# Attention of layer 2: maxima turned in a score bank, away from their own scores; three operand buffers, filled in small parts between the blocks

## The reference

```python
q = q * cos + rot(q) * sin
k = k * cos + rot(k) * sin
g = H // KV
k = jnp.repeat(k, g, axis=1)
v = jnp.repeat(v, g, axis=1)
sc = jnp.einsum('bhqd,bhkd->bhqk', q, k) / jnp.sqrt(jnp.float32(dh))
mask = jnp.where(jnp.tril(jnp.ones((L, L), bool)), 0.0, -1000000000.0)
p = jax.nn.softmax((sc + mask).astype(jnp.float32), -1).astype(q.dtype)
o = jnp.einsum('bhqk,bhkd->bhqd', p, v).transpose(0, 2, 1, 3).reshape(Bsz, L, D)
return o @ o_w + res
```

## Time and profile before

| | |
|---|---|
| median of 3 runs | 6356.77 us |
| the profiled run's own time | 6361.04 us |
| its span | 6359.4 us, mean granted clock 0.826 |
| PE, DVE, ACT, POOL busy | 4190.6, 3786.9, 2670.5, 2605.6 us |
| input stage of attention | about 3564 to 3646 us of the span |
| attention | about 3646 to 4520 us |

### The profile page before, as it was taken

The page is one execution under the profiler, slowest core; times in us unless marked ns, Lnnn a source line. Parts: engine busy times, 40 slices in busy tenths (PEclk is TensorE's granted clock), DMA queues, the critical chain, the costliest instruction groups (busy, mean ns, idle before and its releaser), DMA issues. The chain is left out here.

```text
span 6359.4 us, 49945 instructions
## 1 busy us (share of the span) xinstructions
PE 4190.6 (66%) x13472; PEld 1927.0 (30%) x13472; DVE 3786.9 (60%) x5402; ACT 2670.5 (42%) x3917; POOL 2605.6 (41%) x1948
## 2 busy tenths in 40 slices
PE   4443686095236883788888657777877667777774
PEld 1111233074123551233333333333332222222221
DVE  6999642012322222699999633333436669999987
ACT  3442331031105771566665323333426545454443
POOL 2665001602521004599999200000000057878775
PEclk7776787597558996899999878887888889888897
DMA  1000002121121101344444122222020033333334
GB/s 39 9 9 7 8 0 87 51 68 45 61 102 44 38 31 55 107 154 150 153 153 143 65 30 32 32 31 30 1 71 12 28 106 115 116 118 115 116 114 139
DMA packets 153467, 442.82 MB, mean 70 GB/s; under 512 B 27558, under 2 KB 51048, under 8 KB 149408
## 3 DMA queue, kind: packets, MB, share of 16 engines
q1 hardware_dynamic: 135264, 395.43, 20.4%
q0 software_dynamic: 17984, 44.91, 2.0%
HBM read 363.65 MB, written 77.07 MB: 69 GB/s over the span
## 5 line engine op out<-in xcount | busy, mean ns | idle before, releaser
L1498 ACT ACTIVATE mb_h<-m_dt,m_a_neg 128x512 f32<-128x512 f32 x1024 | 660.7, 681 | 678.5 <-DVE m_hc L1615 578.9
L1376 PE MATMUL mb_y<-m_hc,m_diag_y 128*128 128x512 f32 x1024 | 574.8, 698 | 261.4 <-DVE m_hc L1615 149.5
L1606 DVE TENSOR_TENSOR_SCAN mb_h<-mb_h,m_u 128x1024 f32<-128x1024 f32 x320 | 733.8, 2293 | 8.9
L1568 POOL TENSOR_TENSOR m_u<-m_bsb,m_xs 128x1024 f32<-128x1024 f32 x256 | 598.0, 2357 | 30.7 <-DVE mb_h L1606 30.7
L1568 POOL TENSOR_TENSOR m_u<-m_bsb,m_dtx 128x1024 f32<-128x1024 f32 x256 | 596.1, 2361 | 27.8 <-DVE mb_h L1606 26.6
L1376 PE MATMUL mb_y<-m_hc,w_common 128*128 128x512 f32 x1024 | 513.2, 641 | 136.9 <-DVE m_hc L1615 77.7
L2067 DVE TENSOR_REDUCE at_mx<-at_ps_s 128x4 f32<-128x512 f32 (+1 forms) x256 | 245.1, 957 | 523.7 <-PE at_ps_s L1866 523.6
L1555 POOL TENSOR_TENSOR m_hc<-m_hs,m_csb 128x1024 f32<-128x1024 f32 x192 | 452.2, 2355 | 244.0 <-DVE m_hs L1606 244.0
L1606 DVE TENSOR_TENSOR_SCAN m_hs<-mb_h,m_u 128x1024 f32<-128x1024 f32 x192 | 437.6, 2279 | 1.8 <-POOL m_u L1568 1.8
L1615 DVE TENSOR_TENSOR m_hc<-mb_h,m_csb 128x1024 f32<-128x1024 f32 x320 | 391.8, 1224 | 4.7 <-issue 0.4
L1376 PEld LDWEIGHTS mb_y<-m_hc,m_diag_y 128*128 128x128 f32 x1024 | 202.4, 213 | 622.4 <-DVE m_hc L1615 251.5
(11 more groups left out here) (461 smaller groups left out, 8902.5 us busy)
## 6 DMA issues: line engine op xcount, KB each, us to landing
m_bsb<-bc_rows SPq DMA_DIRECT2D x256, 512.0 KB, 4.8
m_csb<-bc_rows SPq DMA_DIRECT2D x256, 512.0 KB, 4.0
at_q<-q_parts SPq DMA_DIRECT2D x144, 128.0 KB
x_slots<-r1zeros SPq DMA_DIRECT2D x8, 1024.0 KB, 10.0
xg_xg<-x_slots SPq DMA_DIRECT2D x32, 256.0 KB, 2.6
y_slots<-xg_yo POOLq DMA_DIRECT2D x32, 256.0 KB, 2.3
kept_x<-r SPq DMA_DIRECT2D x2, 4096.0 KB, 12.9
x_slots<-r2zeros SPq DMA_DIRECT2D x8, 1024.0 KB, 10.0
```

Source lines behind the costliest of these rows:

```text
L1376: mm = nc.tensor.matmul(ps_y[:, h], weight, hc[:, q % RING, s], start=False, stop=g == GROUPS - 1 and s == SG - 1)
L1498: ins = nc.scalar.activation(ps_h[:, q % 2, s], dt[:, i % 2, h], ACT.Exp, scale=a_neg[:, n:n + 1])
L1568: nc.gpsimd.tensor_tensor(u[:, q % RING], bsb[:, n % RING], dtx[:, i % 2, h].unsqueeze(1).broadcast_to([P, SG, TILE]), ALU.mult).then_inc( ...
L1606: V.tensor_tensor_scan(flat(to), flat(ps_h[:, q % 2]), flat(u[:, q % RING]), 0.0, ALU.mult, ALU.add).then_inc(h_ready, 1)
```

## The change

`q9` and `k9` are made outside both stages, with three buffers in place of two. The fill of `k9` and the first fetch go into `attention_inputs`: the fetch in three parts of six transfers, behind the stores of tiles 6, 7 and 8. In `attention` a fetch is always issued in such parts. The first part of fetch 1 comes before all, the other two after the row transfers of blocks 0 and 1. Fetch j follows in three parts after the rows of blocks 4j - 7, 4j - 6 and 4j - 5.

The maxima are turned into the first bank of `ps_s` instead of `misc`. Each block's are turned 6 units before its first unit. The scores of an odd block are made at units 0, 1, 3 and 4 of the block two before it (before: 1, 3, 5, 7). `turn` now waits, for an even block, until VectorE has read the scores of key head 0 of the next block, which lay in that bank; and the next scores to go into that bank (key head 2 of the next block after an even block's turn, key head 0 after an odd block's) wait for ScalarE's copy. The waits that `misc` had forced on `turn`, `to_tokens`, `to_heads` and `project` go.

```diff
+ATT_PARTS = 9 * DH
+ATT_BUFS = 3
+def fetch_parts(sp, q9, k9, q_d, k_d, j, loaded, parts):
+    s = j % ATT_BUFS
+    for a in parts:
+        at = slice(3 * a * DH, 3 * (a + 1) * DH)
+        q_src = q_d[j, :, a].rearrange("(h d) t -> d h t", d=DH)
+        for b in range(3):
+            sp.dma_start(q9[at.start + b * DH:at.start + (b + 1) * DH, s], q_src).then_inc(loaded, 16)
+        k_src = k_d[j // 4, j % 4 * 32:j % 4 * 32 + 32, a].rearrange("(g d) t -> d g t", d=DH)
+        for b in range(3):
+            sp.dma_start(k9[(3 * b + a) * DH:(3 * b + a + 1) * DH, s], k_src).then_inc(loaded, 16)
@@ attention_inputs: vector, first instruction
+            V.memset(k9[64:96].rearrange("p j g t -> p (j g t)"), 1.0).then_inc(filled, 1)
...
@@ attention_inputs: sync, inside the loop over i
+                if 6 <= i < 9:
+                    if i == 6:
+                        sp.wait_ge(filled, 1)
+                        sp.wait_ge(k_out0, 16)
+                        sp.wait_ge(q_out0, 16)
+                    fetch_parts(sp, q9, k9, q_d, k_d, 0, loaded, range(i - 6, i - 5))
+            sp.wait_ge(loaded, 16 * 18)
...
@@ attention
-    scores_at = {first[n] + (2 * g + 1 if n % 2 else g): (n + 2, g) for n in range(BLK - 2) for g in range(NKV)}
-    turn_at = {first[n - 1] if n % 2 else first[n - 2] + 4: n for n in range(2, BLK)}
-    turn_at[first[0]] = 1
+    scores_at = {first[n] + (g + g // 2 if n % 2 else g): (n + 2, g) for n in range(BLK - 2) for g in range(NKV)}
+    turn_at = {first[n - 2] + 6: n for n in range(2, BLK)}
...
-        ps_m = misc[:, 0:64].bitcast(BF16)
+        ps_m = ps_s[:, 0, 0, 0:64].bitcast(BF16)
-        q9 = sb("q9", [P, 2, NH, TILE], BF16)
-        k9 = sb("k9", [P, 2, NKV, TILE], BF16)
...
-            return n // 4 % 2, n % 4 * P, n % 4 // 2 * T
+            return n // 4 % ATT_BUFS, n % 4 * P, n % 4 // 2 * T
@@ scores
-                    pe.wait_ge(loaded[slot], (n // 8 + 1) * LOAD)
+                    if n:
+                        pe.wait_ge(loaded[slot], (n // 4 - 1) // ATT_BUFS * LOAD + LOAD)
+                if n >= 2 and g == (2 if n % 2 else 0):
+                    pe.wait_ge(nm_copied, n)
@@ turn
-                if n == 1:
+                if n == 0:
+                    pe.wait_ge(max_ready, 2 * NKV)
+                elif n == 1:
                     pe.wait_ge(nm_copied, 1)
-                if n % 2 and n >= 3:
-                    pe.wait_ge(x_done, n - 2)
-                if n % 2 == 0 and n >= 2:
-                    pe.wait_ge(on_ready, n - 2) if n >= 4 else pe.wait_ge(nm_copied, n)
+                elif n % 2 == 0 and n + 1 < BLK:
+                    pe.wait_ge(max_ready, (n + 1) * NKV + 1)
@@ to_tokens, to_heads, project
-                if n % 2 and n + 2 < BLK:
-                    pe.wait_ge(nm_copied, n + 3)
-                if n % 2 == 0:
-                    pe.wait_ge(oh_ready, n) if n else pe.wait_ge(nm_copied, 3)
-                if n == BLK - 1:
-                    pe.wait_ge(x_done, n)
+                if n:
+                    pe.wait_ge(x_done if n % 2 else oh_ready, n)
-                if n % 2 and n + 3 < BLK:
-                    pe.wait_ge(nm_copied, n + 4)
-                if n % 2 and n + 1 < BLK:
-                    pe.wait_ge(on_ready, n + 2)
...
@@ sync
-            fetch(0)
-            fetch(1)
+            fetch_parts(sp, q9, k9, q_d, k_d, 1, loaded[1], range(1))
             for n in range(BLK):
                 slot, col, _row = place(n)
                 sp.wait_ge(nm_copied, n + 1)
-                if n >= 8:
-                    sp.wait_ge(c_ready, last[n - 8] + 1)
+                if n >= 4 * ATT_BUFS:
+                    sp.wait_ge(c_ready, last[n - 4 * ATT_BUFS] + 1)
                 for a in range(3):
                     sp.dma_start(q9[PARTS + a:PARTS + a + 1, slot, :, col:col + P], nmt[a * NH:(a + 1) * NH, n % 2])\
                         .then_inc(less[n % 2], 16)
-                if n % 4 == 1 and 4 < n and n // 4 + 1 < NT:
-                    fetch(n // 4 + 1)
+                if n < 2:
+                    fetch_parts(sp, q9, k9, q_d, k_d, 1, loaded[1], range(n + 1, n + 2))
+                j = n // 4 + 2
+                if n % 4 and j < NT:
+                    if n % 4 == 1 and j >= ATT_BUFS:
+                        sp.wait_ge(c_ready, last[(j - ATT_BUFS) * 4 + 3] + 1)
+                    fetch_parts(sp, q9, k9, q_d, k_d, j, loaded[j % ATT_BUFS], range(n % 4 - 1, n % 4))
```

More of the change, by code:

```diff
@@ L1658, with attention_inputs @@
 QPK = NH // NKV
-def attention_inputs(nc, w, h, q_d, k_d, v_all):
+ATT_PARTS = 9 * DH
[10 more added lines that the diff above has]
+            sp.dma_start(k9[(3 * b + a) * DH:(3 * b + a + 1) * DH, s], k_src).then_inc(loaded, 16)
+def attention_inputs(nc, w, h, q_d, k_d, v_all, q9, k9):
     D = 4
@@ L1676, in attention_inputs @@
         (block, q_in, k_in, v_in, q_turned, k_turned, q_added, q_part, q_less, q_split, k_added, k_part, k_less, k_split,
-         v_done, q_out0, q_out1, q_out2, q_out3, k_out0, k_out1) = ctx.enter_context(phase(
+         v_done, filled, q_out0, q_out1, q_out2, q_out3, k_out0, k_out1, loaded) = ctx.enter_context(phase(
              nc, "q_in k_in v_in q_turned k_turned q_added q_part q_less q_split k_added k_part k_less k_split "
-             "v_done q_out0 q_out1 q_out2 q_out3 k_out0 k_out1"))
+             "v_done filled q_out0 q_out1 q_out2 q_out3 k_out0 k_out1 loaded"))
         q_out = (q_out0, q_out1, q_out2, q_out3)
@@ L1791, in _, with attention @@
                 sp.wait_ge(done, NT // 4 // 2 * 16)
-def attention(nc, w, q_d, k_d, v_all, x):
+def attention(nc, w, q_d, k_d, v_all, q9, k9, x):
     BLK = N // P
-    PARTS = 9 * DH
+    PARTS = ATT_PARTS
     RANK = PARTS + 3
@@ L1837, in attention @@
         eyeb = sb("eyeb", [P, QPK, P], BF16)
-        (block, consts, filled, loaded0, loaded1, less0, less1, v_filled, s_ready, max_ready, chain, split, turned, nm_copied,
+        (block, consts, filled, loaded0, loaded1, loaded2, less0, less1, v_filled, s_ready, max_ready, chain, split, turned, nm_copied,
          c_ready, exp_ready, v_ready, ov_ready, tok_ready, rc_ready, on_ready, heads_ready, oh_ready, out_ready,
          x_done) = ctx.enter_context(phase(
-             nc, "consts filled loaded0 loaded1 less0 less1 v_filled s_ready max_ready chain split turned nm_copied "
+             nc, "consts filled loaded0 loaded1 loaded2 less0 less1 v_filled s_ready max_ready chain split turned nm_copied "
              "c_ready exp_ready v_ready ov_ready tok_ready rc_ready on_ready heads_ready oh_ready out_ready x_done"))
-        loaded, less = (loaded0, loaded1), (less0, less1)
+        loaded, less = (loaded0, loaded1, loaded2), (less0, less1)
         LOAD = 16 * 18
         def place(n):
-            return n // 4 % 2, n % 4 * P, n % 4 // 2 * T
+            return n // 4 % ATT_BUFS, n % 4 * P, n % 4 // 2 * T
         @block.tensor
@@ L1905, in values @@
                 for g in range(NKV):
-                    mm = nc.tensor.matmul(ps_v[32 * g:32 * g + 32], vt[:, place(n)[0], n % 4 // 2 * 2 + kb, g], pt[:, (u + g) % 8],
+                    mm = nc.tensor.matmul(ps_v[32 * g:32 * g + 32], vt[:, n // 4 % 2, n % 4 // 2 * 2 + kb, g], pt[:, (u + g) % 8],
                                           start=kb == 0, stop=kb == n % 2)
@@ L1943, in _ @@
             turn(0)
+            turn(1)
             for u in range(STEPS):
@@ L1976, in _ @@
             copy_less(0)
+            copy_less(1)
             for u in range(STEPS):
@@ L2023, in _ @@
         def _(sp):
-            sp.wait_ge(filled, 2)
-            def fetch(j):
-                s = j % 2
-                if j >= 2:
-                    sp.wait_ge(c_ready, last[j * 4 - 5] + 1)
-                for a in range(3):
-                    for b in range(3):
-                        at = slice((3 * a + b) * DH, (3 * a + b + 1) * DH)
-                        sp.dma_start(q9[at, s], q_d[j, :, a].rearrange("(h d) t -> d h t", d=DH)).then_inc(loaded[s], 16)
-                        sp.dma_start(k9[at, s], k_d[j // 4, j % 4 * 32:j % 4 * 32 + 32, b].rearrange("(g d) t -> d g t", d=DH))\
-                            .then_inc(loaded[s], 16)
-            fetch(0)
-            fetch(1)
+            fetch_parts(sp, q9, k9, q_d, k_d, 1, loaded[1], range(1))
             for n in range(BLK):
@@ L2054, in _ @@
             V.memset(vt[:].rearrange("p j b g c -> p (j b g c)"), 0.0).then_inc(rc_ready, 1)
-            V.memset(k9[64:96].rearrange("p j g t -> p (j g t)"), 1.0).then_inc(filled, 1)
             V.memset(nm[:].rearrange("p j c -> p (j c)"), 0.0).then_inc(rc_ready, 1)
@@ L2492, in layer2 @@
             v_all = ctx.enter_context(nc.sbuf_tensor("l2_v", [P, NBLK, NKV * DH], F32))
-            attention_inputs(nc, w, h, q_d, k_d, v_all)
-            attention(nc, w, q_d, k_d, v_all, xn)
+            q9 = ctx.enter_context(nc.sbuf_tensor("at_q9", [P, ATT_BUFS, NH, TILE], BF16))
```

(3 more changed lines are left out.)

## The result

The changed kernel took 6106.23 us (median of 4 runs, 6087.62 to 6118.62), the one before on the same chip 6353.99 us: a ratio of 0.9613 (95% interval 0.9576 to 0.9649). The forecast was 6108 us.

A forecast was written before the change was run, and what follows sets the result against it. TensorE's waits for maxima rows and POOL, and its low clock, were taken to bound attention. 37.5 + 105 + 62 + 43 + 1 = 248 us off 6361.0 gave 6113 for the profiled run; forecast 6108 us, range 6060 to 6190.

The forecast's parts named there:

- Term A: Attention's start: first fetch and fill moved earlier save 41.5 us, less 4 us at the input stage's end: -37.5 us.
- Term B: TensorE's waits for maxima rows behind fetches: 119.8 us go, 8 and 7 us of new waits come: -105 us.
- Term C: Turns of the maxima: block pair at full clock falls from 19.33 to 17.3 us, 2.0 us x 31: -62 us.
- the 0.57: Wait in us per pair for ScalarE's copy of the turned maxima, before the next scores in that bank.
- Term D: TensorE's low clock and restarting in attention: 74.4 us falls to 31 us, 1.0 us kept per pair: -43 us.
- Rival 1: TensorE's clock stays full in nearly all pairs, the remaining 31 us go too: 6077 us; chance 17%.
- Rival 2: TensorE's clock falls in every pair, costing 108 us instead of 31: 6185 us; chance 12%.
- Rival 3: Row transfers pass the fetch data ahead of them on the queue: 6093 us; chance 10%.
- the 15 us of new waits: New waits for rows: 8 us at attention's start and 7 us before odd blocks in the steady state.
- Rival 4: The stall moves: a third per group stays uncovered before odd blocks' rows, 104 us instead of 7: about 6205 us; 8%.
- rival 5: Slower: each of 45 thirds delays the next block's rows, 333 us against 248 gained: about 6440 us; chance 3%.

The follow-up runs named there:

- experiment 5: Changed kernel with the first fetch, whole, and the fill of `k9` back at the start of attention: 6122.45 us, ratio 0.9635.
- experiment 3: Changed kernel with each fetch from the third on issued whole, 18 transfers, three buffers kept: 6217.58 us, ratio 0.9784.
- experiment 4: Changed kernel with two operand buffers in place of three, fetches still in thirds: 6255.74 us, ratio 0.9834.
- experiment 6: Changed kernel with the turned maxima kept in bank `misc` and the waits it needs, new places of scores and turns kept: 6096.39 us, ratio 0.9576.
- experiment 8: Changed kernel with fetches cut by weight, six transfers of fetch 1 also in the input stage: 6071.66 us, ratio 0.9552; run again, 6090.52 us.
- experiment 2: Changed kernel with turns, their bank and the places of the scores put back as before: 6177.92 us, ratio 0.9723.
- experiment 1: Kernel before with the new places of scores and turns and the new bank, two buffers and whole fetches kept: 6299.35 us, ratio 0.9913.

## Why the prediction came out right, step by step

**Term A, the start (-37.5 forecast, -40.8 measured).** The chain was as told, and 2.4 of the 3.3 us that were off lie in one place: I counted 4 us for a later end of the input stage. The last stores there were issued 79.8 us after the stage's first matmul, for 78.2 before: 1.6 us. The stores of tiles 8 to 10 landed 10 to 13 us after their issue, for 2.3 before, and ScalarE waited for such stores three times, 4.7, 4.6 and 0.6 us; nearly all of that was made up by the end. What experiment 5 corrects is the naming of causes, not the size: 28 us are the early fetch's, 13 mostly the small parts'.

**Term B, waits for rows (-105 forecast, -105.1 measured).** Both halves hold. At the start I counted 8 us, and there were 3.68 + 1.47 = 5.2; in the steady state 7 us, and there were 14.7 - 5.2 = 9.5, in eleven waits of 0.3 to 1.3 us in front of blocks 4m + 3, where the slack was said to be thinnest. One was 2.8 us too high and the other 2.5 too low, so that the sum meets to 0.1 us is luck. Most of the waits were thus not in the first 50 us, where the prediction looked for them. The jam itself was tested from both sides (experiments 3 and 4).

**Term C, turns (-62 forecast, -74.1 measured).** The mis-sized term. What goes, 2.81 us a pair, was right; of what comes, ScalarE's copy cost 12.2 / 31 = 0.39 us and not 0.57, and the turns waited for POOL only twice, 0.8 us before the first pair and 0.3 us in it, and not 0.25 a pair. 2.81 - 0.39 - 0.01 = 2.41, and 2.39 was measured. The working of the 0.57 was off too: 0.6 + 0.27 + 0.1 less the 0.22 us it names is 0.75; counted from the end of a `scores_t` of 0.39 us it is 0.58. The estimate of 2.7 us for reduction and split against 2.5 us of work was too close to a tie to be given a price. The cause, too, was told too narrowly: the prediction does not part place from bank, and experiment 6 gives nearly all to the place.

**Term D, clock (-43 forecast, -38.3 measured).** Right in size; the reason was only partly right. I kept 1.0 us a pair for low stretches that come without a stall. In the profile of the changed kernel most of them came with one: past the first 80 us of attention six of the eight low stretches begin at a wait for rows, of only 0.8 to 1.3 us, as in the windows above: TensorE was busy 2.36 of 3.4 us up to 3808.8, and then the clock is 0.50 for 13.7 us. Five waits of the same kind (at 3773.7, 3848.7, 4039.7, 4114.6 and 4183.6; 0.3 to 0.9 us) had no fall behind them. The other two profiles of this kernel are less clear: over all three, 13 of 30 such waits had a fall, and 12 of 25 low stretches began elsewhere. With the late rows taken away (experiment 8), low clock went from 85, 96 and 58 us to 27 and 44 us. How much of that hung on the rows is not shown: experiment 6 kept them and had 44 us, experiment 2 had none of them past the start and 92 us. The falls that stayed in experiment 8 begin, but for one at the start, within 2.5 us of two waits for ScalarE, of 0.67 and 0.43 us, at one place of a pair. The Trainium skill, TensorE: Matmul & The Clock Gate, section HAM oscillation, describes matmul loops whose waits for data re-throttle TensorE, and its section A second HAM failure mode says that short idle places between groups of matmuls do so too. The traces agree with the second by the falls that stayed; for the first they show that a wait for data of about 1 us is sometimes followed by a fall and sometimes not, 13 times of 30.

**Rivals.** Rival 1 (no low clock, 6077) did not happen. Experiment 8 came near its time, with 6072 us in one set and 6091 in the other, but with low clock left and with waits for rows gone. Rival 2 did not happen: 15 pairs ran at full clock throughout. Rival 3, rows that pass the data ahead of them: as the prediction reads the Trainium skill (DMA: Bandwidth & Descriptors, Queues, rings and completion order), the 15 us of new waits would have been none; they were 14.7, and with 18 transfers ahead 120.6. The rule that the rows land only when the fetch's data have ended was told too simply, though. TensorE needs all three row transfers of a block. Behind a whole fetch one of the three landings that the profile counts for them comes 2.3 to 3.6 us after its issue, with the fetch still under way, and the two others after 11 to 17 us. It is so behind every whole fetch of the kernel before and of experiments 1 and 3; in the earlier trace rows the 3.4 is such a first landing and the 14.0 a last one. Rival 4's place was right and its size was not: 9.5 us, not 104. Nothing of rival 5 was seen.

## What to carry to other kernels

A small transfer that something waits for should have its bulk neighbours cut by what lands between it and its use, and cut unevenly where the slots are uneven: here equal thirds left 9.5 us of waits in the profile of the changed kernel, which parts by weight took away, and low clock was less too (36 us on average against 80), in part for a reason that stays open. Cutting and a spare buffer belong together; each alone only moved the wait. Where a faster stretch runs towards a transfer with a fixed end, its gain turns into a longer wait; what shortens such a stretch is an earlier start of the transfer, and the faster work itself is to be judged by the stretches without one. Before a result is moved to another bank, try its new place with the old bank: here the place brought 2.28 us a pair and the bank 0.11.

## What the hardware did that was not expected

Six of eleven waits of at most 1.3 us were followed, in the profile of the changed kernel, by 3.4 to 13.7 us of TensorE at half clock, and a pair with such a wait took up to 23.6 us, 6.7 more than at full clock; the five others had nothing behind them. And two waits for one bank nearly cancelled two others (0.11 us of difference between banks, where 1.6 to 3 had been expected): with the bank `misc`, TensorE waited 0.93 us ahead of a turn, and the 0.67 us for an exponential that the changed kernel had one unit later was gone.
